# Layer 1's router: the first 64 slot scatters wait for the scatter three places ahead instead of two

## The reference, cut to what matters

```python
logits = x @ router_w                       # 2048 tokens, 32 experts
scores = sigmoid(logits)
# 4 of 8 groups by their two best scores, then the best K = 8 experts among them
_, top_k_index = top_k(masked, K)
tkw = take_along_axis(scores, top_k_index); tkw = tkw / tkw.sum(-1) * ROUTED_SCALE
xs = repeat(x, K, axis=0)[argsort(top_k_index.reshape(-1))]   # rows sorted by expert
down = ragged_dot(silu(ragged_dot(xs, w_gate)) * ragged_dot(xs, w_up), w_down)
routed = (down[unsort].reshape(T, K, H) * tkw[..., None]).sum(axis=1)
shared = silu(x @ sw_gate) * (x @ sw_up) @ sw_down
return routed + shared
```

## Time and profile before

| | us |
|---|---|
| median of 3 runs | 3120.46 |
| lowest and highest | 3118.14, 3126.93 |
| the profiled execution | 3133.18 |
| span of its profile | 3131.5 |

### The profile page before, as it was taken

The page is one execution under the profiler, slowest core; times in us unless marked ns, Lnnn a source line. Parts: engine busy times, 40 slices in busy tenths (PEclk is TensorE's granted clock), DMA queues, the critical chain, the costliest instruction groups (busy, mean ns, idle before and its releaser), DMA issues. The chain is left out here.

```text
span 3131.5 us, 34748 instructions
## 1 busy us (share of the span) xinstructions
PE 2768.3 (88%) x9569; PEld 1263.4 (40%) x9572; DVE 1433.1 (46%) x2766; ACT 773.1 (25%) x1190; POOL 1366.4 (44%) x960
## 2 busy tenths in 40 slices
PE   5887975799999887689999998972999999999997
PEld 2343431344444333233333334431555555555453
DVE  7999999332001232266665647211333333333332
ACT  4746653200000010134334332000111111111111
POOL 2777656133000131136646331465455555455554
PEclk8999999999999998889999998996999999999999
DMA  4333222310300699750474001555766666777654
GB/s 124 114 101 106 76 67 54 112 55 14 113 0 14 231 343 326 207 149 1 128 197 111 1 1 64 213 202 179 159 136 151 150 112 130 191 152 151 132 90 72
DMA packets 303703, 386.00 MB, mean 123 GB/s; under 512 B 51058, under 2 KB 208307, under 8 KB 303602
## 3 DMA queue, kind: packets, MB, share of 16 engines
q1 hardware_dynamic: 212434, 243.23, 25.0%
q0 software_dynamic: 68272, 97.19, 16.1%
q10 hardware_dynamic: 22896, 44.30, 5.2%
HBM read 237.10 MB, written 160.27 MB: 127 GB/s over the span
## 5 line engine op out<-in xcount | busy, mean ns | idle before, releaser
L1859 POOL DMA_INDIRECT out_x<-e_yo,e_dest x318 | 493.1, 1551 | 465.3 <-DMA out_x<-e_yo,e_dest 289.6
L1994 PE MATMUL e_psg<-e_wgu,e_xsT 128*128 x1272 | 580.3, 599 | 3.1 <-SPq L1830 1.9
L285 POOL TENSOR_TENSOR hc<-hs,bcst 128x1024 f32<-128x1024 f32 x128 | 300.7, 2349 | 179.6 <-DVE ps_b L505 171.3
L1994 PEld LDWEIGHTS e_psg<-e_wgu,e_xsT 128*128 128x128 f32 x1272 | 228.9, 190 | 235.7 <-issue 234.1
L630 PE MATMUL ps_y<-hc,ident 128*128 128x512 f32 x512 | 241.0, 609 | 88.0 <-POOL hc L285 87.8
L2010 PE MATMUL e_pso<-e_wd,e_hT 128*128 x636 | 298.9, 592 | 0.7 <-DVE e_hT L1935 0.7
L1940 DVE TENSOR_TENSOR e_h<-e_psg,e_sg 128x256 f32<-128x256 f32 x159 | 67.5, 425 | 502.1 <-ACT e_sg L1880 502.1
L511 DVE TENSOR_TENSOR_SCAN hs<-dA,ps_b 128x1024 f32<-128x1024 f32 x128 | 292.7, 2286 | 7.5 <-ACT dA L415 3.3
L1233 PE MATMUL r_ps_t<-r_wd,r_h 128*128 128x512 f32 x480 | 211.2, 601 | 8.7 <-DVE r_h L982 5.1
L1880 ACT ACTIVATE e_sg<-e_psg 128x256 f32<-128x256 f32 x159 | 60.9, 383 | 638.8 <-PE e_psg L1994 638.8
L415 ACT ACTIVATE dA<-dt,a_neg 128x511 f32<-128x511 f32 x256 | 165.1, 713 | 101.9 <-DVE hs L511 96.8
(11 more groups left out here) (414 smaller groups left out, 3795.8 us busy)
## 6 DMA issues: line engine op xcount, KB each, us to landing
e_xs<-slots_in ACTq DMA_DIRECT2D x159, 272.0 KB, 3.1
slots_in<-zeros SPq DMA_DIRECT2D x160, 256.0 KB, 2.3
bcst<-bc_rows SPq DMA_DIRECT2D x128, 256.0 KB, 4.3
e_wgu<-in_wg SPq DMA_DIRECT2D x32, 512.0 KB, 5.2
e_wgu<-in_wu SPq DMA_DIRECT2D x32, 512.0 KB, 6.2
e_wd<-in_wd SPq DMA_DIRECT2D x32, 512.0 KB, 7.1
e_w<-in_wg SPq DMA_DIRECT2D x11, 1408.0 KB, 16.1
e_w<-in_wu SPq DMA_DIRECT2D x11, 1408.0 KB, 18.1
```

Source lines behind the costliest of these rows:

```text
L285: pool.tensor_tensor(hc[:, it % 2, half(h), :], hs[:, it % 2, half(h), :], bc(bcst[:, q, 1, :], 1, HB), ALU.mult).then_inc(sem["hc"], 1)
L1859: pool.indirect_dma_start(halves, bass.IndirectOffsetOnAxis(dest[:, q, a:a + 1], 0), yo[:, q, a * HC:(a + 1) * HC], None, bounds_check=2 * ...
L1994: j = pe.matmul(ps_g[:, q % 2, :], xsT[:, q % 2, k, :], wgu[:, bass.ds(e % RING, 1), k, :], start=k == 0, stop=k == KH - 1)
```

## The change

A constant CLOSE is 2 in layer 0 and 3 in layer 1; the first NARROW scatters wait for scatter n - CLOSE. So layer 0 is as before; in layer 1 scatters 0 to 63 wait for the landing of the one three places ahead, and scatters 64 to 127 of the one four places ahead, as before. No instruction is added; scatter 2 loses its wait.

```diff
@@ -776,6 +776,7 @@
         LANES = 4
+        CLOSE = 2 if L == 0 else 3
         NARROW = NT * K if L == 0 else NT * K // 2
@@ -874,7 +875,7 @@
                         n = t * K + k
                         lane = n % LANES
-                        ahead_of = n - 2 if n < NARROW else n - LANES
+                        ahead_of = n - CLOSE if n < NARROW else n - LANES
                         if ahead_of >= 0:
                             pool.wait_ge(written[ahead_of % LANES], 16 * (ahead_of // LANES + 1))
```

## The result

The changed kernel takes 3170.86 us in the median of 4 runs (3168.39 to 3175.61), beside 3121.47 us (3118.14 to 3126.93) for the kernel before in 4 runs. The ratio is 1.0152 with a 95% interval of 1.0137 to 1.0167: 1.5% slower, where 1.1% faster was forecast, and outside the range. Its profiled run took 3170.58 us. The profiled run of the kernel before took 3133.18 us, and its scatter 0 comes 13.3 us later than that of the kernel after, for which the change is no cause.

A forecast was written before the change was run, and what follows sets the result against it. The prediction took layer 1's chain of 128 scatters to bound the router stage's end. Loss falling from 50.0 to 15.4 us saves 34.6, so 3120.46 - 34.6 = 3085.9 us, 1.1% faster; range 3079 to 3104 us.

The forecast's parts named there:

- What bounded the kernel: End of layer 1's router stage: the chain of 128 scatters runs about 60 us behind everything else; TensorE idles 70.5 us.
- The interval: Quiet stretches of scatters 0 to 63: 1.285 us per scatter, limited by issue; 17.9 us lost become 0.
- Beside the weights: Scatters beside the weight loads: waiting stays, loss 12.9 us instead of 14.8, between 10.9 and 14.8.
- The 1.5 us beside the second write of x: Loss taken for scatters at distance three beside that write, between 0.55 us at distance four and 3.1 at distance two.
- Who is late next: Stage's end: last scatter near 2123, still 25 us behind TensorE; gains up to about 55 us meet no other end.
- The rivals: Three alternatives: longer landing in quiet stretches (3104 us, chance 0.12), slower (3145, 0.05), no change (about 3120, 0.05).
- The slower one (3145): Scatters before 64: third in flight raises landing to 6.0 us, interval to 2.25; 25 us longer, 3145 us, chance 0.05.
- The third rival: No change, about 3120 us: experts' stage gives the time back, or the chain was not the end; chance 0.05.
- VectorE shutting out GpSimd: Scatters beside VectorE's two-port work 0.14 to 0.25 us longer; at most 16 us over 64 scatters, leaving a gain of 19.

The follow-up runs named there:

- the last experiment: Changed kernel with distance three up to scatter 79, then four, and every eighth scatter from 32 to 72 waiting for the one before; 3110.3 us, ratio 0.9959.

## Why the prediction was wrong

- **What bounded the kernel, right.** The end of the stage was the chain of scatters; where TensorE stays free (the last experiment but its tail, and the one with pauses up to 80), a shorter chain shortens the kernel.
- **The interval, right.** 1.285 us with "issue" ahead, as taken from the second half. The first 64 took 97.1 us where some 98 were forecast.
- **Beside the weights, right.** In the 22.5 us in which the kernel before issued scatters 6 to 12, the kernel after issued 8 (scatters 9 to 17, 1943.34 to 1965.86). That is a loss of 22.5 - 8 x 1.285 = 12.2 us, where 12.9 was taken between 10.9 and 14.8. The 1.5 us beside the second write of x were never put to the test: that write waits for TensorE and was issued only at 2079.11, 149.4 us after scatter 0 (70.1 before), beside scatters at distance four. The chain to the last scatter became 31.1 us shorter, where 34.6 was forecast; the rest was lost behind scatter 64.
- **Who is late next, wrong: this is the step that failed.** The prediction gave TensorE's end the value that it had before, 25 us ahead of the last scatter, and allowed "a gain of up to about 55 us" before another end was met. It took for granted that TensorE's work beside the scatters keeps its length whatever the pace of the scatters. It became 108 us longer. The rows could not rule that out: the earlier trace rows hold 132 us of TensorE's work beside scatters at 2.07 us, and only 24 us of it beside scatters at 1.285. The second half was a good model of what scatters do at that pace, and nearly no model of what they do to others, since for most of it TensorE was idle. The prediction used it for both.
- **The rivals, wrong in their mechanism.** The slower one (3145) let the landing grow to 6.0 us and the chain with it. The chain did not grow. None of the rivals had another engine slowed by the scatters. The third rival found nothing in the rows against the gain, which is the same omission.
- **VectorE shutting out GpSimd,** which the prediction weighed as a price on the scatters: the 128 scatters of after take 988 ns each in the mean, beside 0.98 us undisturbed, so all of them together lost 1 us and not 16.

What the shared limit is stays open. Shown is: it starts with the pace of the scatters and not with their bytes, rows or number in flight, it is charged per instruction of TensorE, weight load or matmul; it takes 17 to 26 us to build up (less with twice as many instructions), and it sits between 1.685 and 1.285 us a scatter. In the slow stretch the trace's own records of semaphore updates run thin, but they do so before it as well, and in the run with pauses without it. Either the path of semaphore updates is full, or the path that records what happens is, and holds TensorE up. That TensorE pays for instructions which update no semaphore speaks for the second; that VectorE's instructions do not get longer in the slow stretch (0.69 us throughout) speaks against a path that holds up every engine alike, though GpSimd's register moves do grow, later. Neither is shown: every execution here came with its span and granted clock, and no kernel was run with less recording, so these two were not told apart. The Trainium skill (NOTIFIC — the notification-queue block, Overflow: three behaviours, one of which stalls the engine) says that the block's internal queue always pushes back on its producers rather than lose a record. That would fit a delay that builds up over some 20 us and is charged per instruction; but the count above shows records missing as well, which that rule does not give, and also where TensorE is on time; no run here tests it.

## What to carry to other kernels

When a stretch of the trace is the model for a faster pace, look at what else ran in it: it prices the engine that you speed up, and says nothing of engines that were idle there. When a chain off TensorE gets shorter, check whether its denser issue now lies beside TensorE's work, and read that work's completion from its consumers, not from TensorE's own starts. Here short pauses in the scatter stream, and keeping its gapless part for the time when TensorE is nearly done, beat both the wide spacing and none. All of this was measured with the profiler's recording on; whether an execution without it is slowed at all, no run here tells.

## What the runs showed of the hardware

- In these recorded executions, indirect scatters issued by GpSimd every 1.285 us slow TensorE to one pair of weight load and matmul per 2.80 us, 1.40 for each of the two, for 512 and for 256 columns alike (0.43 us a pair otherwise for 512), until the scatters end. At 1.685 and at 2.00 us a scatter they do not.
- The slow state has a delay: about 26 us after the stream closed up in the kernel with distance four from scatter 32 (21 after a pause of 0.5 us in it), 22 to 24 with distance four throughout, 21 after the last pause of the version with the pieces together and of the one with pauses up to 80, 20 in the one with pauses up to 64, 17 to 19 in the kernel after and the two in which a stream of 1.7 to 1.8 us went before, and 9 to 14 with twice as many matmuls. In the kernel before it was 24 us without any slowing. So it isn't one fixed time; what came before counts, as for a load that adds up.
- VectorE's and ScalarE's own instructions keep their length in the slow stretch (0.69 and 0.60 us as elsewhere; for ScalarE it holds a single one), and the scatters keep their 0.98 us. The register moves in GpSimd's queue grow from 29 to some 700 ns, in the kernel after from 2059.5 on, some 75 us after TensorE turned slow.
- Starts of TensorE in the trace run ahead of what is finished. In the kernel after some 20 matmuls of L1215 start between 2039.71 and 2049 at full speed, while the additions that wait for earlier ones come 22.4 us apart.
- Records of semaphore updates can be missing from a trace: 408 of the scatters' 2048 are there in the kernel after, and all 2048 in the kernel before. With pauses up to 80, 858 of the 1344 that were sent in the first 150 us are there, and TensorE is on time up to then.
